# A decoder layer on one core: VectorE's next rows and mask in front of the keys' low parts, GpSimd's bias additions behind these, and tile 0's second normalisation turned on TensorE

## The chip, the core and the metric

The kernel runs on one core of a Trainium2 chip. The time is device microseconds of one execution, from its launch to its end. The core's engines work side by side, each through its own queue in order: TensorE (PE, matrix products into the eight PSUM banks; its weight loads are listed as PEld), VectorE (DVE), ScalarE (ACT), GpSimd (POOL) and SyncE (SP, which issues DMAs). They wait for one another through semaphores.

## What is computed

A decoder layer of one block-wise self-attention, one cross-attention and one feed-forward network, on `x` of 4 x 1024 x 512 and a context of 4 x 64 x 512, in fp32:

```python
x = x + self_attention(layernorm(x))        # 512-wide head, causal inside blocks of 128 rows
x = x + cross_attention(layernorm(x), ctx)  # 16 heads of 32, 64 keys, silu in place of softmax, mask
x = x + ffn(layernorm(x))                   # gelu(h @ w1 + b1) @ w2 + b2, 2048 wide

# cross-attention
q = query @ Wq.T + bq;  k = key @ Wk.T + bk;  v = value @ Wv.T + bv
scores = where(mask == 0, -1e9, q k^T * SCALE)
out = (silu(scores) @ v) @ Wo.T
```

## The kernel before

**Arithmetic.** Each fp32 operand of a product is kept as two parts, a high part (a copy in the type fp32r, written by ScalarE) and a low part (the value minus the high part, written by VectorE or GpSimd). `product` (lines 53 to 56) is three matrix instructions: high by low, low by high, high by high. So each result in a PSUM bank costs one pass of ScalarE and one of VectorE before TensorE can use it again. In names, `_hi` and `_lo` are the two parts. `*_high` and `*_low` are the functions that write them.

**Stages.** After a set-up stage, the 4096 rows go through both attentions in 8 tiles of 512 rows (`TILES`), then through the feed-forward network in 8 tiles. A tile has four blocks of 128 rows (`NB`) and the 512 columns are four chunks of 128 (`EC`).

**The attention pipeline.** `step(a, b, par)` does the self-attention of tile `a` and the cross-attention of tile `b = a - 1` together. `pipeline` writes `step(0, None, 0)` and `step(1, 0, 1)` out, runs steps 2 to 5 in a hardware loop, writes steps 6 and 7 out, and ends with `last_step(7)`. "The step of tile 2" below means a = 2, b = 1. The order on each engine is the order in which its `step` is written.

**TensorE's step.** The queries of tile b (`queries`, reading the second normalisation as `attn`); two of the four pairs of cross scores; value rows 0; the self scores (lines 1139 and 1141, which wait for the first masked cross score of tile b, `s2_masked`, and for all of `q_lo`); value rows 1; cross outputs 0 and 1 (waiting for `attn_lo`); cross scores 2 and 3; the transposes of the probabilities (line 1161); value rows 2 and 3; the probabilities times the values; cross outputs 2 and 3; the output projection; and the rows `y` of the next tile (`y_rows(a + 1, m)`, reading the next tile's first normalisation as `zT`). In step 0 the keys of all batches stand in the place of tile b's work.

**VectorE's step.** At its start, `start_step` writes the low parts of the keys (`kb_lo`, line 860), after ScalarE has written `kb_hi` (line 711). `rows_ahead` normalises the rows of tile a + 1 into `zn` (line 145). `q_low` writes the queries' low parts (line 842), `mask_now` turns the mask into floats (line 894), `values_low` writes the values' low parts (`vb_lo`, line 900), and `mask_scores` scales and masks the cross scores (line 850). ScalarE then takes `silu` of each masked score, and GpSimd subtracts (`silu_low`, line 653, `attn_lo`).

**Turning a normalisation.** TensorE needs the normalised rows with rows and columns exchanged. The kernel turns squares of 32 x 32 on VectorE (`dve.transpose`, lines 878 and 889) and moves the squares to their places by 16 DMAs (`move_squares`, line 262): for the first normalisation all are issued by SP, for the second 8 by SP and 8 by ScalarE. For tile 7's second normalisation TensorE itself does it (`transposed_rows`, line 151, 16 transposes by the identity matrix). Both parts of the second normalisation go into `attn` (lines 781 and 883).

**GpSimd's step.** The bias additions `x_in + bout_row` (line 667, four per tile), then `silu_low` for eight scores, then the reciprocal roots of the two normalisations (`norm_rstd`, lines 138 and 140). The additions start when the rows ahead are normalised (`z1_ready`); in the step of tile 1 they wait also for the keys' low parts (`kv_ready`).

## Time and profile before

| | us |
|---|---|
| median of 3 runs | 1257.65 |
| lowest and highest run | 1256.87, 1259.6 |
| the profiled execution's own time | 1257.62 |
| its span (first to last instruction) | 1255.8 |
| TensorE busy | 1230.2 |
| VectorE busy | 700.8 |
| ScalarE busy | 489.6 |
| GpSimd busy | 254.1 |
| mean granted TensorE clock, share of full speed | 0.994 |

All times in the views are microseconds from the start of the span of one profiled execution. The profiled execution is 0.03 us from the median, so what is worked out on the trace can be set against the median as it is. The attention steps run from about 40 us to 555 us, the feed-forward tiles from there to the end. In a timeline row, several instructions of a kind in a row are merged with their count, and the brackets give the idle time of the engine before the row and the instruction that ended it.

### The profile page before, as it was taken

The numbers are of one execution on the slowest core, as the hardware profiler recorded it, in microseconds if no ns is written. First come the engines' busy times: TensorE is split into PE (matmuls) and PEld (weight loads), VectorE is DVE, ScalarE is ACT, GpSimd is POOL, SyncE is SP. The second block draws the span as 40 slices with busy tenths as digits, with TensorE's granted clock in tenths as the row PEclk, the third lists the DMA queues.
The fourth block names the chain that finished last, engine by engine and source line by source line (L and its number), as shares of the span: only waits on it lengthen the run. The fifth ranks groups of instructions, "written<-read, shape, count | busy, mean of one in ns | idle before, by whom it ended". The sixth has DMA issues, their size and how long they took to land.

```text
span 1255.8 us, 15452 instructions
## 1 busy us (share of the span) xinstructions
PE 1230.2 (98%) x5560; PEld 1019.8 (81%) x5560; DVE 700.8 (56%) x1266; ACT 489.6 (39%) x888; POOL 254.1 (20%) x226
## 2 busy tenths in 40 slices
PE   9979999999999999999999999999999999999998
PEld 7867878787878788878888888888888888888887
DVE  8777878887888876855733433424424333334211
ACT  7336464646464648453332232222222222323221
POOL 2223232323232332159402001001001020010000
PEclk9999999999999999999999999999999999999999
DMA  8451515151515140325120010020100200100000
GB/s 298 148 138 33 156 35 155 33 158 36 153 34 154 38 118 13 126 92 178 50 67 1 1 68 1 1 67 0 64 3 0 67 0 0 67 0 0 35 1 33
DMA packets 76789, 82.22 MB, mean 65 GB/s; under 512 B 8257, under 2 KB 47169, under 8 KB 76737
## 3 DMA queue, kind: packets, MB, share of 16 engines
q1 hardware_dynamic: 68672, 77.90, 20.0%
q10 hardware_dynamic: 8064, 3.67, 1.3%
q8 instruction: 27, 0.44, 0.1%
q14 instruction: 26, 0.20, 0.1%
HBM read 48.51 MB, written 18.35 MB: 53 GB/s over the span
## 4 chain that ended last, share of the span: by engine, by line
PE 55%; DVE 0%; issue 0%; DVEq 0%
PE bank L54 18%; PE bank L55 18%; PE bank L56 18%; DVE resid L1403 0%; DVEq L1402 0%
## 5 line engine op out<-in xcount | busy, mean ns | idle before, releaser
L1393 DVE TENSOR_TENSOR hid_lo<-gelu_out,hid_hi 128x512 fp32r<-128x512 f32 x128 | 97.3, 760 | 405.0 <-ACT gelu_out L1357 405.0
L1353 ACT ACTIVATE hid_hi<-bank,small 128x512 fp32r<-128x512 f32 x128 | 88.0, 688 | 499.2 <-PE bank L56 499.2
L54 PE MATMUL bank<-zT,w_parts 128*128 128x512 f32 x656 | 255.5, 389 | 1.7 <-DVE zT L864 0.9
L56 PE MATMUL bank<-zT,w_parts 128*128 128x512 f32 x656 | 255.3, 389 | 0.0
L55 PE MATMUL bank<-zT,w_parts 128*128 128x512 f32 x656 | 255.3, 389 | 0.0
L54 PE MATMUL bank<-w2p_hi,hid_lo 128*128 128x512 f32 x512 | 199.3, 389 | 0.0
L55 PE MATMUL bank<-w2p_lo,hid_hi 128*128 128x512 f32 x512 | 199.3, 389 | 0.0
L56 PE MATMUL bank<-w2p_hi,hid_hi 128*128 128x512 f32 x512 | 199.2, 389 | 0.0
L54 PEld LDWEIGHTS bank<-zT,w_parts 128*128 128x128 f32 x656 | 123.1, 188 | 28.1 <-issue 2.6
L55 PEld LDWEIGHTS bank<-zT,w_parts 128*128 128x128 f32 x656 | 123.2, 188 | 25.4
L56 PEld LDWEIGHTS bank<-zT,w_parts 128*128 128x128 f32 x656 | 123.1, 188 | 25.5
L138 POOL TENSOR_SCALAR ve<-mv 128x4 f32<-128x4 f32 x24 | 7.7, 321 | 524.7 <-DVE mv L133 351.0
L56 PEld LDWEIGHTS bank<-w2p_hi,hid_hi 128*128 128x128 f32 x512 | 96.2, 188 | 19.9
L54 PEld LDWEIGHTS bank<-w2p_hi,hid_lo 128*128 128x128 f32 x512 | 96.2, 188 | 19.9
L55 PEld LDWEIGHTS bank<-w2p_lo,hid_hi 128*128 128x128 f32 x512 | 96.1, 188 | 19.9
L653 POOL TENSOR_TENSOR attn_lo<-scratch,attn_hi 128x512 fp32r<-128x512 f32 x64 | 81.6, 1296 | 139.3 <-ACT scratch L705 139.2
L1357 ACT ACTIVATE gelu_out<-bank,small 128x512 f32<-128x512 f32 x128 | 87.2, 682 | 0.0
L1390 DVE STREAM_TRANSPOSE z_cols<-zn 32x512 f32<-32x512 f32 x112 | 78.7, 703 | 4.2
L1317 POOL TENSOR_TENSOR resid<-resid,b_row 128x512 f32<-128x512 f32 x32 | 45.2, 1443 | 116.2 <-DVE zn L145 116.2
L692 ACT ACTIVATE yv_hi<-bank 128x512 fp32r<-128x512 f32 x32 | 18.9, 597 | 112.4 <-issue 85.0
L820 DVE TENSOR_TENSOR yv_lo<-bank,yv_hi 128x512 fp32r<-128x512 f32 x64 | 43.3, 685 | 32.4 <-ACT yv_hi L692 26.3
L704 ACT ACTIVATE attn_hi<-scratch 128x512 fp32r<-128x512 f32 x64 | 40.0, 624 | 40.7 <-DVE scratch L850 40.2
(156 smaller groups left out, 2039.9 us busy)
## 6 DMA issues: line engine op xcount, KB each, us to landing
x_in<-in_x SPq DMA_DIRECT2D x32, 256.0 KB, 4.8
x_dram<-resid SPq DMA_DIRECT2D x32, 256.0 KB, 2.4
raws<-in_w SPq DMA_DIRECT2D x32, 256.0 KB, 3.2
resid<-x_dram SPq DMA_DIRECT2D x32, 256.0 KB, 3.7
out_dram<-resid SPq DMA_DIRECT2D x32, 256.0 KB, 2.1
raws<-in_x SPq DMA_DIRECT2D x28, 256.0 KB, 3.5
z_cols<-raws SPq DMA_DIRECT2D x112, 64.0 KB, 2.0
z_cols<-scratch SPq DMA_DIRECT2D x56, 64.0 KB, 2.1
```

What stands on the lines that cost most here:

```text
L54: pe.matmul(out_ap, lhs[1], rhs[0], start=start, stop=False)
L55: pe.matmul(out_ap, lhs[0], rhs[1], start=False, stop=False)
L56: return pe.matmul(out_ap, lhs[0], rhs[0], start=False, stop=stop)
L653: pool.tensor_tensor(attn[1][:, j % 4, :], act_in[:, j % 3, :], f(attn[0][:, j % 4, :]), ALU.subtract).then_inc(attn_lo, 1)
L692: act.activation(yv[0][:, m, :], bank[y_bank(a, m)][:, :], ACT.Copy).then_inc(y_hi, 1)
L704: act.activation(attn[0][:, j % 4, :], act_in[:, j % 3, :], ACT.Silu)
L820: dve.tensor_tensor(hl[1][:, m, :], bank[from_bank][:, :], f(hl[0][:, m, :]), ALU.subtract).then_inc(made, 1)
L1317: pool.tensor_tensor(resid[:, slot, i, :], resid[:, slot, i, :], b2_row[:, :], ALU.add).then_inc(x2_biased, 1)
L1353: act.activation(hid[0][:, c % 4, :], bank[4 + c % 3][:, :], ACT.Gelu, bias=b1_col[:, c:c + 1])
L1357: act.activation(gelu_out[:, c % 2, :], bank[4 + c % 3][:, :], ACT.Gelu, bias=b1_col[:, c:c + 1]).then_inc(hid_full, 1)
L1390: dve.transpose(*squares(TURNS_AT_ONCE * (c - FIRST_TURN) + n, z3_cols)).then_inc(z3_turned, 1)
L1393: dve.tensor_tensor(hid[1][:, c % 4, :], gelu_out[:, c % 2, :], f(hid[0][:, c % 4, :]), ALU.subtract).then_inc(hid_lo, 1)
```

## The change

Four things change.

1. In VectorE's step for every tile b, `rows_ahead` (while there is a next tile) and `mask_now` come ahead of `start_step`, and `values_low` comes between `q_low(2)` and `q_low(3)`. Before, this held for the step of tile 1 alone as far as `rows_ahead` and the mask go, and there `values_low` stood behind the first three masked scores.
2. GpSimd's bias additions wait in every step for the keys' low parts.
3. Tile 0's second normalisation is turned by 16 transposes on TensorE, after `y_rows(1, 1)`, into banks 7, 5, 0 and 1. ScalarE and VectorE write its two parts from there. The turning on VectorE and the 16 DMAs of SP and ScalarE go away for this tile. The semaphore counts of the moves and turns shift by one tile.
4. In step 0 `z1_low` (the low parts of tile 1's first normalisation) comes before the statistics of the second normalisation.

GpSimd's step:

```diff
                             if more(a):
                                 pool.wait_ge(z1_ready, NB * (a + 2))
-                                if b is not None and first(b):
-                                    pool.wait_ge(kv_ready, HEADS_PER_CHUNK)
+                                if b is not None:
+                                    pool.wait_ge(kv_ready, len(BLOCKS) * b + HEADS_PER_CHUNK)
```

ScalarE's step, after the first normalisation's high parts (SP's step has the same condition around its half of `move_squares`):

```diff
-                                act.wait_ge(z2_turned, NB * (a + 1))
-                                move_squares(act, scratch, range(QUADS // 2, QUADS), z2_moved)
+                                if not first(a):
+                                    act.wait_ge(z2_turned, NB * a)
+                                    move_squares(act, scratch, range(QUADS // 2, QUADS), z2_moved)
                                 y_high(a + 1, 0)
                                 y_high(a + 1, 1)
-                                act.wait_ge(z2_moved, MOVES * (a + 1))
-                                for c in range(EC):
-                                    act.activation(by_blocks(attn[0], c), by_quads(c), ACT.Copy).then_inc(z2T_hi, 1)
+                                if first(a):
+                                    for i in range(NB):
+                                        act.wait_ge(z2T_done, i + 1)
+                                        act.activation(attn[0][:, :, cols(i)], chunks(bank[FIRST_Z2_BANK[i]][:, :]),
+                                                       ACT.Copy).then_inc(z2T_hi, 1)
+                                else:
+                                    act.wait_ge(z2_moved, MOVES * a)
+                                    for c in range(EC):
+                                        act.activation(by_blocks(attn[0], c), by_quads(c), ACT.Copy
+                                                       ).then_inc(z2T_hi, 1)
```

VectorE, `rows_ahead` and the step:

```diff
                         def rows_ahead(n, b):
+                            if b is not None and first(b):
+                                dve.wait_ge(z2T_done, NB)
                             norm_rows(dve, lambda i: ahead[i], mv1, rstd1, ln1, n)
...
                             if b is not None:
-                                if first(b):
+                                if more(a):
                                     rows_ahead(a + 1, b)
-                                    mask_now(b)
+                                mask_now(b)
                                 start_step(b)
-                                if more(a) and not first(b):
-                                    rows_ahead(a + 1, b)
-                                q_low(b, 0)
-                                q_low(b, 1)
-                                if not first(b):
-                                    mask_now(b)
-                                q_low(b, 2)
-                                if not first(b):
-                                    values_low(b)
+                                for m in range(EC - 1):
+                                    q_low(b, m)
+                                values_low(b)
                                 q_low(b, EC - 1)
                                 dve.wait_ge(mask_ready, b + 1)
                                 for j in range(3):
                                     mask_scores(b, j)
-                                if first(b):
-                                    values_low(b)
...
+                            if first(a):
+                                for c in range(EC):
+                                    z1_low(1, c)
                             dve.wait_ge(x1_ready, NB * (a + 1))
...
                                 norm_rows(dve, lambda i: x1_rows(i, par), mv2, rstd2, ln2, a)
-                                turn2(a, b)
-                                if b is not None:
+                                if not first(a):
+                                    turn2(a, b)
...
-                                for c in range(EC):
-                                    z2_low(a, c)
+                                if first(a):
+                                    for i in range(NB):
+                                        dve.wait_ge(z2T_hi, i + 1)
+                                        dve.tensor_tensor(attn[1][:, :, cols(i)],
+                                                          chunks(bank[FIRST_Z2_BANK[i]][:, :]),
+                                                          f(attn[0][:, :, cols(i)]), ALU.subtract).then_inc(z2T_lo, 1)
+                                else:
+                                    for c in range(EC):
+                                        z2_low(a, c)
```

TensorE's step, at its end, with the new table of banks:

```diff
+FIRST_Z2_BANK = (7, 5, 0, 1)
...
                                 for m in range(EC):
                                     y_rows(a + 1, m)
+                                    if first(a) and m == 1:
+                                        pe.wait_ge(keys_out, EC)
+                                        for i in range(NB):
+                                            transposed_rows(pe, z2_ready, a, i, FIRST_Z2_BANK[i], z2T_done)
```

The order on VectorE at the start of the step of tile 6; `zn` are the rows ahead, `qo` the queries, `scratch` the masked scores. Before:

```order
L860 TENSOR_TENSOR kb_lo<-keys_now,kb_hi 32x4x64 x4
L145 TENSOR_SCALAR zn<-raws,mv,rstd 128x512 x4
L842 SCALAR_TENSOR_TENSOR qo_hi<-bank,bias_cols,qo_hi 64x512
L842 SCALAR_TENSOR_TENSOR qo_lo<-bank,bias_cols,qo_lo 64x512
L842 SCALAR_TENSOR_TENSOR qo_hi<-bank,bias_cols,qo_hi 64x512
L842 SCALAR_TENSOR_TENSOR qo_lo<-bank,bias_cols,qo_lo 64x512
L894 TENSOR_SCALAR mask_i<-mask_i 128x512
L842 SCALAR_TENSOR_TENSOR qo_hi<-bank,bias_cols,qo_hi 64x512
L842 SCALAR_TENSOR_TENSOR qo_lo<-bank,bias_cols,qo_lo 64x512
L900 TENSOR_TENSOR vb_lo<-values_now,vb_hi 64x4x32 x4
```

The same place now:

```order
L146 TENSOR_SCALAR zn<-raws,mv,rstd 128x512 x4
L904 TENSOR_SCALAR mask_i<-mask_i 128x512
L869 TENSOR_TENSOR kb_lo<-keys_now,kb_hi 32x4x64 x4
L851 SCALAR_TENSOR_TENSOR qo_hi<-bank,bias_cols,qo_hi 64x512
L851 SCALAR_TENSOR_TENSOR qo_lo<-bank,bias_cols,qo_lo 64x512
L851 SCALAR_TENSOR_TENSOR qo_hi<-bank,bias_cols,qo_hi 64x512
L851 SCALAR_TENSOR_TENSOR qo_lo<-bank,bias_cols,qo_lo 64x512
L851 SCALAR_TENSOR_TENSOR qo_hi<-bank,bias_cols,qo_hi 64x512
L851 SCALAR_TENSOR_TENSOR qo_lo<-bank,bias_cols,qo_lo 64x512
L910 TENSOR_TENSOR vb_lo<-values_now,vb_hi 64x4x32 x4
```

The four row normalisations and the mask moved from behind the keys' low parts to ahead of them; in both orders the last `q_low` and the masked scores follow.

The order on ScalarE at the end of step 0; `yv_hi` are tile 1's rows `y`, `attn_hi` the second normalisation of tile 0. Before:

```order
L769 ACTIVATE raws<-bank,bias_cols 128x4x64 x4
L262 DMA z_cols<-scratch 32x4x128 x8
L692 ACTIVATE yv_hi<-bank 128x512 x2
L781 ACTIVATE attn_hi<-z_cols 128x512 x4
L692 ACTIVATE yv_hi<-bank 128x512 x2
```

Now:

```order
L770 ACTIVATE raws<-bank,bias_cols 128x4x64 x4
L693 ACTIVATE yv_hi<-bank 128x512 x2
L784 ACTIVATE attn_hi<-bank 128x4x128 x4
L693 ACTIVATE yv_hi<-bank 128x512 x2
L712 ACTIVATE kb_hi<-keys_now 32x4x64 x8
```

The eight DMAs left the queue, and the four copies read PSUM banks that TensorE's transposes fill.

## Rows read from the trace of the kernel before

**Rows 1.** The page, busy time of TensorE: busy us, share of span, instructions.

```profile
PE 1230.2 (98%) x5560; PEld 1019.8 (81%) x5560; DVE 700.8 (56%) x1266; ACT 489.6 (39%) x888; POOL 254.1 (20%) x226
```

**Rows 2.** Waits of TensorE: waited-for instruction, us in total, times, longest.

```profile
PE bank L1139 <- DVE scratch L850: 9.8, 5, 2.0
```

**Rows 3.** Timeline of TensorE: start, us, instruction, idle time before it in brackets.

```profile
76.54 0.47 PE L54 MATMUL bank<-zT,w_parts 128*128 128x512 f32 x1 [0.87 <-DVE zT L864]
...
93.82 0.80 PE L54 MATMUL bank<-attn_hi,w_parts 128*128 128x512 f32 x1 [6.15 <-DVE attn_lo L883]
...
119.70 0.50 PE L54 MATMUL bank<-attn_hi,vb_lo 128*128 128x512 f32 x1 [0.44 <-POOL attn_lo L653]
...
124.55 0.63 PE L1161 MATMUL bank<-ident,scratch 128*128 128x128 f32 x4 [1.34 <-DVE yv_lo L820]
...
175.82 0.38 PE L1139 MATMUL bank<-zT,yv_hi 128*128 128x256 f32 x1 [1.99 <-DVE scratch L850]
```

**Rows 4.** Stretches of TensorE: window, length, busy (count), granted clock, DMA, GB/s.

```profile
93.82:97.82 4.00, 4.00 (x9) 0.50 0.00 0
175.82:181.12 5.30, 5.30 (x33) 0.68 0.10 37
239.14:242.88 3.74, 3.74 (x32) 1.00 0.16 59
301.08:306.38 5.30, 5.30 (x32) 0.68 0.10 39
485.99:489.63 3.64, 3.64 (x33) 1.00 0.04 13
516.52:518.18 1.66, 1.66 (x17) 1.00 0.83 309
```

**Rows 5.** Timeline of VectorE, step of tile 2.

```profile
159.08 0.69 DVE L820 TENSOR_TENSOR yv_lo<-bank,yv_hi 128x512 fp32r<-128x512 f32 x1 [0.69 <-ACT yv_hi L692]
162.60 1.76 DVE L860 TENSOR_TENSOR kb_lo<-keys_now,kb_hi 32x256 fp32r<-32x256 f32 x4 [2.83 <-ACT kb_hi L711]
164.39 1.92 DVE L145 TENSOR_SCALAR zn<-raws,mv,rstd 128x512 f32<-128x512 f32 x4
...
172.16 1.24 DVE L900 TENSOR_TENSOR vb_lo<-values_now,vb_hi 64x128 fp32r<-64x128 f32 x4
...
174.99 1.89 DVE L850 SCALAR_TENSOR_TENSOR scratch<-bank,mask_i 128x512 f32<-128x512 f32 x3
```

**Rows 6.** Timeline of ScalarE, step of tile 2.

```profile
159.08 3.49 ACT L711 ACTIVATE kb_hi<-keys_now 32x256 fp32r<-32x256 f32 x8
...
167.48 0.68 ACT L716 ACTIVATE qo_lo<-bank,bias_cols 64x512 fp32r<-64x512 f32 x1
...
170.05 0.68 ACT L716 ACTIVATE qo_lo<-bank,bias_cols 64x512 fp32r<-64x512 f32 x1
```

**Rows 7.** Timeline of GpSimd, step of tile 2.

```profile
166.48 5.23 POOL L667 TENSOR_TENSOR x_in<-x_in,bout_row 128x512 f32<-128x512 f32 x4 [9.60 <-DVE zn L145]
```

**Rows 8.** Timeline of VectorE and GpSimd, end of tile 0's step.

```profile
68.47 2.48 DVE L987 TENSOR_TENSOR resid<-bank,x_in 128x512 f32<-128x512 f32 x4
...
73.92 2.47 DVE L864 TENSOR_TENSOR zT<-z_cols,zT 128x512 fp32r<-128x512 f32 x4
76.31 1.91 DVE L145 TENSOR_SCALAR zn<-resid,mv,rstd 128x512 f32<-128x512 f32 x4
...
74.75 1.33 POOL L140 TENSOR_TENSOR rstd<-ve,minus_half 128x4 f32<-128x4 f32 x1
```

**Rows 9.** Timeline of VectorE and GpSimd, step of tile 1.

```profile
96.89 0.43 DVE L894 TENSOR_SCALAR mask_i<-mask_i 128x512 f32<-128x512 int32 x1
...
111.02 4.17 DVE L900 TENSOR_TENSOR vb_lo<-values_now,vb_hi 64x128 fp32r<-64x128 f32 x4
...
111.17 3.87 POOL L653 TENSOR_TENSOR attn_lo<-scratch,attn_hi 128x512 fp32r<-128x512 f32 x3 [6.93 <-ACT scratch L705]
```

**Rows 10.** Timeline of ScalarE, tile 7's second normalisation.

```profile
517.15 2.07 ACT L156 ACTIVATE zT<-bank 128x512 fp32r<-128x512 f32 x4 [8.00 <-PE bank L151]
```

More of the change, by code:

```diff
@@ L629, in step @@
                                 load_kv(0)
-                            if more(a):
-                                sp.wait_ge(z2_turned, NB * (a + 1))
+                            if more(a) and not first(a):
+                                sp.wait_ge(z2_turned, NB * a)
                                 move_squares(sp, scratch, range(QUADS // 2), z2_moved)
@@ L642, in last_step @@
                         def last_step(b):
-                            sp.wait_ge(z2_moved, MOVES * (TILES - 1))
+                            sp.wait_ge(z2_moved, MOVES * (TILES - 2))
                             for c in range(STAGES):
@@ L785, in step @@
                                 for i in range(NB):
-                                    transpose_high(act, i, BLOCK_BANK[i], z2T_done, z2T_hi, 0)
+                                    transpose_high(act, i, BLOCK_BANK[i], z2T_done, z2T_hi, 1)
                         def last_step(b):
@@ L873, in turn2 @@
                             dve.wait_ge(z2_ready, NB * (a + 1))
-                            if b is not None:
-                                dve.wait_ge(attn_lo, PAIRS * (b + 1))
+                            dve.wait_ge(attn_lo, PAIRS * (b + 1))
                             dve.nop(nofuse=True)
@@ L999, in step @@
                             if more(a):
-                                for c in range(EC):
-                                    z1_low(a + 1, c)
+                                if not first(a):
+                                    for c in range(EC):
+                                        z1_low(a + 1, c)
                                 norm_rows(dve, lambda i: x1_rows(i, par), mv2, rstd2, ln2, a)
-                                turn2(a, b)
-                                if b is not None:
+                                if not first(a):
+                                    turn2(a, b)
                                     for i in range(3):
@@ L1015, in step @@
                                 y_low(a + 1, 1)
-                                for c in range(EC):
-                                    z2_low(a, c)
+                                if first(a):
[5 more added lines that the diff above has]
+                                else:
+                                    for c in range(EC):
+                                        z2_low(a, c)
                                 y_low(a + 1, 2)
@@ L1032, in last_step @@
                             start_step(b)
-                            dve.wait_ge(z2T_done, NB)
+                            dve.wait_ge(z2T_done, 2 * NB)
                             norm_rows(dve, lambda i: x_in[:, i, :], mv3, rstd3, ln3, 0)
```

## The prediction

> **What bounds the kernel now.** I read the page first. TensorE is busy 1230.2 of 1255.8 us [rows 1], so only its idle time, and time at a lower clock, can be won. Next come its waits: the longest entry is 9.8 us in 5 waits for `scratch` of line 850, the masked cross scores [rows 2]. The timeline places the others: one wait of 6.15 us for `attn_lo` of line 883, the low part of tile 0's second normalisation, 0.87 us ahead of tile 1's rows `y`, and 0.44 and 1.34 us in the step of tile 1 [rows 3]. All other idle time lies in the set-up, in tile 0's transposes of probabilities, in the last step and behind the feed-forward tiles, where nothing is changed. Last I read the clock by stretches. After the 6.15 us of waiting, nine products take 4.00 us at a granted clock of 0.50, which is the 1.2 GHz level. The self scores behind the waits of tiles 2 and 4 take 5.30 us at a mean of 0.68. The same instructions behind the wait of tile 3 take 3.74 us at 1.00 (2.4 GHz), and in tile 7, with no wait, 3.64 us [rows 4]. Tiles 5 and 6 read like tile 3.
>
> **Why the five waits are there.** In the step of tile 2, TensorE is free at 175.82 - 1.99 = 173.83 and the first masked score starts at 174.99 [rows 3, 5]. It comes late since VectorE is a full queue from 162.60 on: low parts of the keys, then 1.92 of rows ahead, `q_low` in eight halves with the mask among them, 1.24 of `vb_lo`. Ahead of 162.60 it idles for 2.83 us, waiting for ScalarE's `kb_hi` [rows 5, 6].
>
> **Part 1, rows ahead and mask first.** They go into that hole: 1.92 for the rows and 0.43 for the mask, which is its price with GpSimd idle [rows 5, 9]. That is 2.35 of 2.83, so `kb_lo` still starts at 162.60 and ends at 164.36. What it needs, the rows' factors from GpSimd, is in place earlier than 159.8: GpSimd has been idle for 9.60 us when its bias additions start at 166.48, since 156.9 [rows 7]. Behind `kb_lo` stand six halves of `q_low`. Two of them lie between 172.16 + 1.24 = 173.40 and 174.99, so one takes 0.79 [rows 5]. They wait for ScalarE's halves too: the sixth of these ends at 167.48 + 0.68 = 168.16, at 0.7 each the first at 164.6 [rows 6]. So VectorE's six end at 164.6 + 6 x 0.79 = 169.3. `vb_lo` takes 1.24, to 170.6, ScalarE's last half is there at 170.05 + 0.68 = 170.73 [rows 6], and the last two `q_low` end at 172.1 to 172.3. The first masked score then starts near 172.2 in place of 174.99, and is done 0.7 later, at 172.9. TensorE comes at 173.83. The wait of 1.99 is gone with about 0.9 to spare, in five steps: **9.8 us**. Everything behind it on VectorE, ScalarE and GpSimd is earlier by about 2.8, TensorE by 2.0, so no later wait of these steps can open that was closed before: in the undisturbed steps of tiles 3, 5 and 6 TensorE waits nowhere else.
>
> **Part 2, GpSimd's additions behind the keys.** They start at 164.4 in place of 166.48, since what they wait for is done earlier than before. They end at 164.4 + 5.1 = 169.5 [rows 7], ahead of the first silu. What they can hit is `vb_lo`: 1.24 alone, but 4.17 with GpSimd's subtractions beside it [rows 5, 9]. `vb_lo` starts at 169.3 and the additions end at 169.5, so I take 0.2 to 0.7 of delay, within the 0.9 to spare. Zero on the path.
>
> **Part 3, clock.** With no wait the self scores of tiles 2 and 4 cost 3.64 in place of 5.30, and those of tiles 3, 5 and 6 3.64 in place of 3.74 [rows 4]: 2 x 1.66 + 3 x 0.10 = **3.6 us**.
>
> **Part 4, tile 0's second normalisation.** The wait of 6.15 goes. TensorE pays 16 transposes: 1.66 for the same instructions in tile 7 [rows 4], and 0.1 for the slower product behind them: net **4.4 us**. Is it ready in time? `z1_low` (2.47) now stands right behind the residual additions, which end at 68.47 + 2.48 = 70.95, and ends at about 73.4. Statistics, aggregates and GpSimd's factors follow, all later by `z1_low`'s 2.4. The factors ended at 74.75 + 1.33 = 76.08 and so end at 78.5, and the normalised rows (1.91) lie at 78.6 to 80.5 [rows 8]. TensorE starts the rows `y` at 76.54 - 0.87 = 75.67, with 48 products to 93.82 - 6.15 = 87.67, or 0.232 each, so two chunks end at 81.2. The rows are there, with 0.7 to spare. The transposes end at 82.9. ScalarE copies 4 x 0.5 (2.07 [rows 10]) to about 84.1, VectorE subtracts (2.5, as in [rows 8]) to about 86.7, and TensorE wants them at 87.67 - 0.87 + 1.76 = 88.56. Slack 1.9. ScalarE no longer issues eight DMAs there, SP neither; nothing stands behind these in SP's queue but the next tile's. Nine products at half clock (4.00) become 9 x 0.232 = 2.09: **1.9 us**.
>
> **Part 5, `z1_low` first.** The rows of `zT` are ready at 73.4 and TensorE is free at 75.67: **0.9 us**.
>
> **Part 6, the step of tile 1.** Its `vb_lo` took 4.17 beside GpSimd's subtractions, and held up the turning, the self scores' masking and so on to the wait of 1.34 [rows 3, 9]; the other steps, with `vb_lo` early, have no such wait, nor the one of 0.44. From 88.56 on this step runs as that of tile 2 does: **1.8 us**.
>
> **Sum.** 9.8 + 3.6 + 4.4 + 1.9 + 0.9 + 1.8 = 22.4. Against the profiled execution, 1257.62 - 22.4 = 1235.2; the median is the same within 0.03, so I say **1235.3 us**. The feed-forward part does not change.
>
> **Bounds.** The transposes: from 1.66, if the product behind them loses nothing, to 1.66 + 1.9, if nine products behind them run at half clock. The first product behind a wait took 0.47 to 0.80 [rows 3] where a row of products further on takes less; that each wait gone gives back some 0.08 more is not in the sum and is worth up to 0.5. The scores' wait: from zero to 0.5 us in each of six steps, if `vb_lo` is held longer than I take. The spread of the runs before is -0.8 to +1.9 us.
>
> **Rivals.**
>
> A. *The transposes lower the clock.* At their stretch in tile 7 the clock was 1.00 [rows 4], and TensorE is busy before and behind. For it speaks that waits of 2.0 were followed by half clock in two of five cases. Price: the nine products behind them, 1.9, or these and the transposes at half clock, 1.9 + 1.7: 1237.2 to 1238.9. Chance 0.08. The Trainium skill ("TensorE: Matmul & The Clock Gate", Part 4: PE-mode transpose) says that the full clock does not engage for transposes, which would make this rival the likely one; the 1.00 in tile 7 is against it.
>
> B. *The port contention takes the gain.* If GpSimd's additions and all four `vb_lo` collide, these take 4.17, 2.9 more, the first masked score is done at 175.7 and the waits of 1.9 and the half clock return, now in the step of tile 1 too: 22.4 - 9.8 - 3.6 - 1.9 = 7.1 saved, 1250.5. It takes an overlap of 4 us; I work out 0.2. A part of it, 0.5 to 1 us of wait in six steps, gives 1238 to 1241. Chance 0.10 for both.
>
> C. *Slower: VectorE stands in front of the rows ahead.* `rows_ahead` waits for GpSimd's factors. Now the keys' low parts, the queries' and the scores stand behind it. If the factors come s after 159.8, the first masked score slips by s less 0.5 (hole) less 0.9 (spare). With six such steps the 22.4 are used up at s = 22.4 / 6 + 1.4 = 5.1, that is factors at 164.9 in place of 156.9; at 166 the time is 1257.6 + 6 x 1.1 = 1264. The 2.9 us by which the factors are early speak against it. Chance 0.02.
>
> D. *The gap is not VectorE's.* If the self scores' wait ended by something else, the 13.4 of parts 1 and 3 stay: 1248.7. The row names line 850, and in tile 7, where there are no rows ahead, the same place has no wait [rows 4]. Chance 0.02.
>
> **How the numbers follow.** The forecast has 0.78, and 1233.8 to 1240 holds it, A, and the small half of B: 1233.8 is the sum less 0.8 (the runs), 0.1 (transposes) and 0.5 (first products), 1240 the sum with 0.5 us in six steps and the spread of the runs. A measurement of this kernel tells about 0.2% (2.5 us) from no change. Only C gives slower: 0.02. Same needs B with a clock worse than seen: 0.01. Faster 0.97.
>
> **What would show it.** TensorE's waits have no entry for the masked scores of line 859, and none for the second normalisation of tile 0. The granted clock stays 1.00 from 40 us to the end. On VectorE the rows ahead and the mask start right behind the last `y_low`, `kb_lo` has 0.3 to 0.5 of idle time before it, and the first masked score starts 12.3 behind the end of `y_low` in place of 15.2. The additions of GpSimd start with the end of `kb_lo`. Sixteen transposes stand between the second and third chunk of rows `y`. Wrong would be: `vb_lo` over 2 us in the loop, a wait of TensorE at the transposes, or a new wait behind the masked scores.

## The result, and the profile after

The changed kernel takes **1236.68 us** in the median of 4 runs (1235.93 to 1237.49), beside 1257.72 for the kernel before: a ratio of 0.983 with an interval of 0.982 to 0.9845. The profiled execution took 1236.69, its span 1234.6. Set beside [rows 1], the page begins:

```profile
span 1234.6 us, 15467 instructions
PE 1225.1 (99%) x5576; PEld 1017.9 (82%) x5576; DVE 692.1 (56%) x1262; ACT 489.5 (40%) x888; POOL 250.2 (20%) x226
```

TensorE's view of waits (engine and tile, what ended the wait, microseconds in total, times, longest), which answers [rows 2]:

```profile
PE bank L56 <- issue: 1.7, 2, 0.8
PE bank L470 <- POOL kb_lo L432: 1.3, 1, 1.3
PE bank L55 <- POOL attn_lo L654: 1.0, 2, 0.6
PE bank L55 <- DVE attn_lo L893: 1.0, 1, 1.0
```

The wait for the masked scores (line 859 now) has no entry any more, and neither has tile 0's second normalisation. Two entries are new: `attn_lo` of line 893, once, and `issue`, twice. The second means that TensorE stood and the profile shows nothing that it waited for.

TensorE's timeline, beside [rows 3]: the 16 transposes in tile 0's step, the product behind them, and two of the three new gaps. Brackets hold the idle time ahead and what ended it.

```profile
81.32 1.91 PE L152 MATMUL bank<-ident,zn 128*128 128x128 f32 x16
82.98 0.48 PE L55 MATMUL bank<-zT,w_parts 128*128 128x512 f32 x1
...
208.91 0.50 PE L55 MATMUL bank<-attn_hi,w_parts 128*128 128x512 f32 x1 [0.97 <-DVE attn_lo L893]
...
797.09 0.40 PE L56 MATMUL bank<-zT,w_parts 128*128 128x512 f32 x1 [0.84 <-issue]
```

The third, at 972.19, is like the second, with 0.82. VectorE and then GpSimd in the step of tile 2, the place of [rows 5] and [rows 7]:

```profile
149.53 1.91 DVE L146 TENSOR_SCALAR zn<-raws,mv,rstd 128x512 f32<-128x512 f32 x4
151.63 0.43 DVE L904 TENSOR_SCALAR mask_i<-mask_i 128x512 f32<-128x512 int32 x1 [0.19 <-DVE zn L146]
152.45 1.76 DVE L869 TENSOR_TENSOR kb_lo<-keys_now,kb_hi 32x256 fp32r<-32x256 f32 x4 [0.39 <-ACT kb_hi L712]
...
159.18 1.33 DVE L910 TENSOR_TENSOR vb_lo<-values_now,vb_hi 64x128 fp32r<-64x128 f32 x4
...
162.10 1.89 DVE L859 SCALAR_TENSOR_TENSOR scratch<-bank,mask_i 128x512 f32<-128x512 f32 x3
```

```profile
154.37 5.04 POOL L668 TENSOR_TENSOR x_in<-x_in,bout_row 128x512 f32<-128x512 f32 x4 [7.29 <-DVE kb_lo L869]
```

The values' low parts take 1.33, 0.1 over their 1.24 alone, so GpSimd's additions hardly touch them. The first masked score starts at 162.10 and TensorE starts the self scores at 163.66 without a wait.

**Where the 21.2 us of span went.** The listed idle time undercounts a wait, because the ends of the pipelined products are modelled. So I measured from the start of one group of products to the start of the next. "Attention" is from the first product of tile 0's step (line 336 or 337, at about 40 us) to the first of the feed-forward part (line 578 or 579). "Feed-forward" is from there to the end of the span.

| | before | after | saved | forecast |
|---|---|---|---|---|
| values 0 ahead of the self scores, five steps (4.87, 4.85, 4.86, 4.86, 4.74; now 2.72) | | | 10.6 | 9.8 |
| self scores (5.30 twice and 3.74 three times; now 3.64) | | | 3.6 | 3.6 |
| tile 0: rows `y` and transposes | 17.28 | 12.69 | 4.6 | 4.4 |
| tile 0: queries at half clock | 12.91 | 10.88 | 2.0 | 1.9 |
| tile 0: wait ahead of rows `y` | 1.15 | 0.12 | 1.0 | 0.9 |
| step of tile 1 (0.74, 1.52, 0.16, 0.29) | | | 2.7 | 1.8 |
| end of the step of tile 2 (10.88, now 12.01; queries +0.14) | | | -1.3 | 0 |
| **attention, whole** | 515.57 | 491.91 | 23.7 | 22.4 |
| **feed-forward** | 699.92 | 701.98 | -2.1 | 0 |
| set-up | 40.31 | 40.67 | -0.4 | 0 |

The rows of the attention stretch add up to 23.2; the other 0.5 lies in pieces under 0.12. 23.7 - 2.1 - 0.4 = 21.2.

### The profile page after: what moved, and what is told of

Its sections match the earlier page's. It is cut to its first block, busy times and chain, and to the rows that moved or that the text cites. A ratio compares the mean times of both kernels' runs of the same rounds, so it can differ in the third digit from the quotient of the medians.

```text
span 1234.6 us, 15467 instructions
## 1 busy us (share of the span) xinstructions
PE 1225.1 (99%) x5576; PEld 1017.9 (82%) x5576; DVE 692.1 (56%) x1262; ACT 489.5 (40%) x888; POOL 250.2 (20%) x226
## 3 DMA queue, kind: packets, MB, share of 16 engines
q10 hardware_dynamic: 6912, 3.15, 1.1%
## 4 chain that ended last, share of the span: by engine, by line
PE 56%; DVE 0%; issue 0%; DVEq 0%
PE bank L55 19%; PE bank L57 19%; PE bank L56 19%; DVE resid L1420 0%; DVEq L1419 0%
## 5 line engine op out<-in xcount | busy, mean ns | idle before, releaser
L55 PE MATMUL bank<-w_parts,zT 128*128 128x512 f32 x128 | 51.3, 401 | 0.0
```

The source lines that it names most:

```text
L55: pe.matmul(out_ap, lhs[1], rhs[0], start=start, stop=False)
```

## Experiments

All kernels together: the median, the ratio to the kernel before with its interval, the two stretches as defined above, and the idle gaps of TensorE inside the feed-forward part.

| kernel | median | ratio | attention | feed-forward | gaps |
|---|---|---|---|---|---|
| before | 1257.72 | | 515.57 | 699.9 | none |
| after | 1236.68 | 0.982-0.9845 | 491.91 | 702.0 | 0.84, 0.82 |
| c1_after | 1236.12 | 0.9795-0.9831 | 491.99 | 702.5 | 1.26, 0.94 |
| e1_order_only | 1241.17 | 0.9836-0.9871 | 499.98 | 700.0 | none |
| e2_tile0_only | 1251.65 | 0.9927-0.9961 | 507.97 | 702.4 | 1.01, 0.77 |
| e3_no_gp_wait | 1254.19 | 0.9945-0.9975 | 508.79 | 702.2 | 0.93, 0.85 |
| e4_rows_behind | 1245.14 | 0.9884-0.9917 | 500.21 | 702.1 | 1.01, 0.50 |
| e5_mask_behind | 1238.74 | 0.9836-0.9869 | 493.38 | 702.1 | 0.77, 0.74 |
| e6_values_late | 1254.56 | 0.9965-0.9987 | 509.68 | 702.4 | 1.19, 0.74 |
| e7_transposes_twice | 1235.39 | 0.9806-0.9839 | 493.19 | 700.0 | none |
| e8_z1_low_late | 1237.61 | 0.9812-0.9859 | 492.50 | 702.4 | 1.01, 1.04 |
| b1_value_rows_early | 1236.08 | 0.9797-0.9843 | 491.37 | 702.2 | 0.77, 0.76 |
| b2_shifted | 1233.70 | 0.9783-0.9822 | 490.74 | 700.1 | none |
| b3_both | 1242.21 | 0.9841-0.9885 | 490.85 | 710.6 | 3.15, 2.73 |

**c1_after**: after once more.

> The changed kernel once more. What the first trace had that the prediction had not: a wait of 0.97 us of TensorE for tile 2's second normalisation (208.9), and two idle stretches of 0.84 and 0.82 us in the feed-forward loop that no semaphore ended (795.9 and 971.0), some 3 us in all from start to start. Theory 'of this kernel': the same three stand at the same places and cost the same. Theory 'of the execution': they stand elsewhere, or not at all, and the span differs by what is missing. Time 1236 to 1238 in both.

The new wait came back in the same place (1.05 at 209.42), and the two gaps too. They belong to the program, not to one execution.

**e1_order_only** is before with parts 1, 2 and 6 alone, **e2_tile0_only** has parts 4 and 5 alone.

```diff
-                                if b is not None and first(b):
-                                    pool.wait_ge(kv_ready, HEADS_PER_CHUNK)
+                                if b is not None:
+                                    pool.wait_ge(kv_ready, len(BLOCKS) * b + HEADS_PER_CHUNK)
...
+                                for m in range(EC - 1):
+                                    q_low(b, m)
+                                values_low(b)
```

> The kernel before with VectorE's new order in all steps and GpSimd's wait alone; tile 0's second normalisation goes by VectorE and DMAs as before. Theory of the prediction: the five waits of the self scores go (10.6 us from start to start), their clock loss (3.6), and the two waits in the step of tile 1 (2.3), so 16.5 less than before: 1241.2. TensorE still waits 6.15 us for tile 0's second normalisation, with nine products at half clock. Rival (the waits of tile 1's step hang on tile 0's late start, not on values_low): these stay, 1243.5. Rival (gain given back behind the scores): a new entry of several us in TensorE's waits, 1246 or more.

> The changed kernel with VectorE's old order and GpSimd's old wait; only tile 0's normalisation on TensorE and the earlier z1_low are left. Theory of the prediction: 6.4 + 1.9 + 1.0 less 1.7 for the transposes: 7.6 less than before, 1250.1; the five waits of about 2 us and the two in tile 1's step stay. Rival (the transposes lower the clock): granted clock of 0.5 behind 81 us, 1252. Rival (half clock in two tiles of five hangs on the place in time): the tiles with half clock behind their wait are others than tiles 2 and 4, 1248.5 to 1252 by their number.

The order alone takes 15.6 off the attention stretch (forecast 9.8 + 3.6 + 1.8 = 15.2), tile 0's edits 7.6 (forecast 4.4 + 1.9 + 0.9 = 7.2). The sum, 23.2, is nearly the 23.7 of both, so the two halves add up. That the first lies so near its forecast is partly luck. From start to start, 1.05 of its 15.6 comes from a place without an edit: tile 0's wait is 5.07 in place of 6.15, since the moves ahead of it land earlier. In tile 4's step it loses 1.9 again, to the wait below. The second median is 1.5 over what was expected: it has the gaps of after (2.5 more in its feed-forward part), which tile 0's edit brings and the order does not. Its self scores take 5.31 in tiles 2 and 4 and 3.72 to 3.75 in tiles 3, 5 and 6. So half clock stands in the same two tiles as before, though these run 7.4 us earlier, and the rival of the place in time did not come true.

In e1_order_only one wait for a masked score is left, 0.99 at 291.40, in tile 4's step alone. It starts on VectorE:

```profile
278.48 1.92 DVE L145 TENSOR_SCALAR zn<-raws,mv,rstd 128x512 f32<-128x512 f32 x4 [2.61 <-issue]
```

**e3_no_gp_wait**: after, without GpSimd's wait for the keys' low parts.

```diff
-                                if b is not None:
-                                    pool.wait_ge(kv_ready, len(BLOCKS) * b + HEADS_PER_CHUNK)
```

> The changed kernel without GpSimd's new wait: the bias additions start when the rows ahead are there, beside the mask and the keys' low parts. Theory 'shared port': the mask takes 0.9 in place of 0.43, kb_lo up to 4.2 in place of 1.76, the first masked score slips by up to 2.4, TensorE waits up to 1.4 us in six steps: 1240 to 1246. Rival 'no contention at this place' or 'GpSimd is the one that is held': kb_lo 1.8, the same time as the changed kernel, 1236.7.

Contention it is, but at almost twice the highest price expected (17.5 in the median against 9.3): the attention stretch is 16.9 longer, more than the 15.6 that the new order brings. VectorE, GpSimd and TensorE's waits:

```profile
154.88 1.56 DVE L902 TENSOR_SCALAR mask_i<-mask_i 128x512 f32<-128x512 int32 x1 [0.19 <-DVE zn L146]
156.37 4.82 DVE L867 TENSOR_TENSOR kb_lo<-keys_now,kb_hi 32x256 fp32r<-32x256 f32 x4
161.22 0.74 DVE L849 SCALAR_TENSOR_TENSOR qo_hi<-bank,bias_cols,qo_hi 64x512 fp32r<-64x512 f32 x1
```

```profile
154.87 5.59 POOL L666 TENSOR_TENSOR x_in<-x_in,bout_row 128x512 f32<-128x512 f32 x4 [4.55 <-DVE zn L146]
```

```profile
PE bank L1150 <- DVE scratch L857: 7.6, 6, 1.3
PE bank L1092 <- DVE qo_lo L849: 4.0, 11, 0.4
```

The mask takes 1.56 in place of 0.43 and the keys' low parts 4.82 in place of 1.76: 4.2 more per step, against about 0.9 of spare. TensorE now waits twice in a step, for the queries' low parts (0.3 to 0.4 at a time) and for the masked score (1.3), and loses 2.5 to 3.0 per step from start to start in six steps. I had looked for the first masked score alone.

The Trainium skill ("SBUF — State Buffer", section "SBUF: two separate sides") says that VectorE and GpSimd share one pair of ports, taken for a whole instruction, for VectorE's operations with two inputs in SBUF among them. The rows agree: the keys' low parts, with two such inputs, stretch by 2.7 times, while the queries' halves, with one of their two large inputs in a PSUM bank, take 0.74 to 0.76 with or without GpSimd.

**e4_rows_behind** and **e5_mask_behind**: the two pieces of part 1 put back one at a time.

```diff
-                                if more(a):
-                                    rows_ahead(a + 1, b)
                                 mask_now(b)
                                 start_step(b)
+                                if more(a):
+                                    rows_ahead(a + 1, b)
```

```diff
-                                mask_now(b)
                                 start_step(b)
...
                                 q_low(b, 1)
+                                mask_now(b)
                                 q_low(b, 2)
```

> After, but VectorE's rows ahead stand behind the start of the step's keys' low parts' successors as before the change; the mask stays in front, GpSimd's additions stay behind the keys. If the hole ahead of the keys' low parts is what pays (my Part 1), the 1.92 of rows ahead are back in VectorE's full queue: the first masked score of tile 2 starts about 1.9 to 2.4 later than in after, TensorE waits about 1.0 for it in the five steps of tiles 2 to 6 (half of the 1.99 of before, since the mask's 0.43 and the contention are gone), 5 x 1.0 to 1.2 and up to 2 for a lower clock: 1242 to 1245. If the gain came from GpSimd's additions being moved away alone, there is no wait and the time stays at 1236 to 1237.

> After, but the mask stands again between the second and third half of the queries' low parts; rows ahead stay in front. The mask then runs beside GpSimd's additions and should take 0.9 to 1.5 in place of 0.43. If there are 0.9 of spare ahead of the masked scores as I worked out, the wait for them is 0 to 0.3 in six steps: 1236 to 1238. If there is no spare left, each of six steps loses the whole 0.9 to 1.5: 1242 to 1245.

With the rows ahead behind the keys, VectorE stands 2.50 idle ahead of `kb_lo` again, and TensorE waits 6.4 in six steps for the masked scores (1.26 to 1.47 from start to start in five of them, 0.55 in tile 3's): 8.3 on the attention stretch, and a median of 1245.14, at the upper end of what was expected. So the hole ahead of the keys carries a good half of the order's 15.6. The clock stays at 1.00 behind these waits.

The mask beside the additions takes 0.84 in place of 0.43:

```profile
157.66 0.84 DVE L904 TENSOR_SCALAR mask_i<-mask_i 128x512 f32<-128x512 int32 x1
```

The first masked score then starts 0.83 later, at 162.93. No wait is listed, yet values 0 take 2.79 to 2.91 in place of 2.72 in five of the six steps, and the self scores behind them 3.72 to 3.75 in place of 3.65: 0.2 to 0.3 per step. With smaller pieces the attention stretch is 1.5 longer, and the median is 0.7 over the expected range. Of the delay of 0.83, 0.1 to 0.2 reaches TensorE's start of the self scores, so the spare that I put at 0.9 is about 0.7 (an estimate).

**e6_values_late**: the values' low parts behind three masked scores in all steps, as the step of tile 1 had it before.

```diff
-                                for m in range(EC - 1):
+                                for m in range(EC):
                                     q_low(b, m)
-                                values_low(b)
-                                q_low(b, EC - 1)
...
+                                values_low(b)
```

> After, but the values' low parts (1.33) stand behind the three masked scores, where GpSimd's subtractions of the silu run, in all steps, as in before they stood in the step of tile 1 alone. If two-input operations on VectorE stretch beside GpSimd, they take about 4.2, and the waits of before's step of tile 1 (0.44 and 1.34, 0.60 and 1.52 from start to start) come up in all seven steps with a predecessor: 7 x 1.8 to 2.1, 1249 to 1251. If that step was late for another reason (its place behind tile 0), the time stays at 1236 to 1238.

```profile
166.18 4.19 DVE L910 TENSOR_TENSOR vb_lo<-values_now,vb_hi 64x128 fp32r<-64x128 f32 x4
```

```profile
166.33 3.88 POOL L654 TENSOR_TENSOR attn_lo<-scratch,attn_hi 128x512 fp32r<-128x512 f32 x3 [4.11 <-ACT scratch L706]
```

Here they are 4.19 beside GpSimd's subtractions, and the pair of waits of tile 1's step (0.46 and 1.28) stands in all six steps. That confirms the cause of part 6. The time is above the expectation, which counted seven steps at 1.8 to 2.1: six lose 2.8 to 3.0 each from start to start. The transposes of the probabilities (+0.2) and the value rows behind them (+0.3) are slower too.

**e7_transposes_twice**: tile 0's 16 transposes done twice.

> After, but TensorE does the 16 transposes of tile 0's second normalisation twice, the second set writing the same values again. What transposes cost is 1.66 for sixteen, if the granted clock stays at 1.00 over 32 of them in a row: 1236.7 + 1.7 = 1238.3, nothing waits, since what needs them has 1.9 of slack and loses 1.7. If the clock falls in transposes (rival A), nine products behind them at half clock or these and the transposes: 1240.2 to 1243.5, and the records show 0.50 there.

TensorE by windows (length, busy and count of each engine, then the granted clock, DMA share, GB/s): the 32 transposes, then the 24 products behind them.

```profile
81.92:85.33 3.41, 3.41 (x33) 3.41 (x32) 3.02 (x9) 1.62 (x4) 1.01 (x2) 1.00 0.67 239
85.33:90.90 5.57, 5.57 (x27) 4.59 (x26) 2.78 (x5) 1.64 (x4) 0.26 (x1) 1.00 0.00 0
```

The second set costs 1.75, at a clock of 1.00 (2.4 GHz) in and behind them: rival A is out, and the sentence of the Trainium skill that spoke for it ("TensorE: Matmul & The Clock Gate", Part 4: PE-mode transpose) does not hold for these 32. But the kernel, expected at 1238.3, is no slower than after (1235.39 against 1236.68). The attention stretch is 1.3 longer, and the two gaps of the feed-forward part, where nothing had been touched, are gone. This led to the next kernel.

**b2_shifted**: 32 empty instructions in TensorE's program.

```diff
                                 for m in range(EC):
+                                    if first(a):
+                                        for k in range(8):
+                                            pe.wait_ge(x1_ready, 1 + k % NB)
+                                            pe.nop(nofuse=True)
                                     y_rows(a + 1, m)
```

> After, with 32 empty instructions more in TensorE's program, each with a wait that is already met, eight ahead of each chunk of rows y in tile 0's step. They do nothing; all of TensorE's program behind them stands 32 instructions further on. Seen so far: the feed-forward part (from its first product to the end of the span) takes 699.9 to 700.0 in before, in the kernel with the new order only, and in the kernel with the transposes doubled, and 702.0 to 702.5 with two idle stretches of 0.5 to 1.3 and instruction fetches beside them in the six kernels whose TensorE program is that of after. Theory: what decides is where the loop over the feed-forward tiles stands in the program. Shifted by 32, as with the doubled transposes, it takes 700.0, the two idle stretches are gone, and the time is 1236.5 - 2.1 = 1234.4, plus at most 1 for the empty instructions. Rival: the transposes' doubling helped in another way (less collision of transfers): then 702.1 and 1236.5 to 1237.5.

The fastest kernel: 1233.70 (1232.99 to 1234.35), 2.9 of span below after, where 2.1 were expected. Both gaps are gone, and so is the new wait of 1.0 at the end of tile 2's step. The DMA view around the gap at 797, of after (785 to 812) and then of b2_shifted (784 to 811, the same place in its feed-forward part); the columns are packets, MB, and share of the 16 engines:

```profile
q8 instruction: 4, 0.07, 0.9%
```

```profile
q8 instruction: 1, 0.02, 0.3%
```

Over the whole run q8, which brings instructions, has 27 packets in before and in e1_order_only, 28 in e7_transposes_twice and b2_shifted, and 46 in all the others, whose loop over the feed-forward tiles fetches its code on every pass. The gaps end 264.5 and 439.6 behind the start of the part, 175 apart: that is the length of one pass (two tiles), so there is one behind each jump back to the loop's head. TensorE's branch at the loop's end stands in the view of its line, of b2_shifted and then of after (how often, the least, median and most ns of one, and the first and last start; the last of the three is not taken):

```profile
L1288 PEldq COMPARE_BRANCH  x3: 76/213/233, 788.8 to 1137.0; - x3
L1284 PEldq COMPARE_BRANCH  x3: 83/3475/3507, 789.9 to 1140.1; - x3
```

A jump back takes 0.21 to 0.23 us in the kernels without gaps and 3.3 to 3.9 in all the others. In after, one packet of q8 comes during it (at 790.99) and one ahead of the gap (794.76). TensorE takes the branch 4.0 ahead of the first product of the new pass, which starts at 793.82, so the 3.5 hold up no product there but leave 0.5 of the lead. The gap comes ten products later. It does so in the nine kernels whose loop has the place of after, and two products into the pass in b3_both, whose loop stands 16 instructions (eight products with their weight loads) further on. So the gap keeps its place in TensorE's program, not its place in the loop.

The Trainium skill ("Runtime: NRT & Kernel Launch", section "Instruction fetch mechanics") says that TensorE's instruction memory holds 2048 instructions, filled in blocks of 256 (the packets of q8 are of 16 KB each here), and that a taken branch waits for a fetch when its target is not in the window of two blocks. The 3.3 to 3.9 agree with a wait for a fetch. The two blocks do not agree with the kernels without gaps: between 787 and 1159 in b2_shifted q8 brings nothing, while TensorE jumps back over more than six blocks twice. An estimate from the page's block: the loop has 768 products, as many weight loads and 38 others, 1574 or 6.15 blocks, so by where it starts it touches 7 or 8 of the 8. Counted with the weight loads, the loop stands 33 instructions later in after than in before and in e1_order_only, 49 later in b3_both, and 65 later in b2_shifted and e7_transposes_twice. The two places between are the bad ones, and an eighth block would be touched from 37 places in every 256, which fits. So does the gap's fixed place. If a block ends there, an estimate from the products and the shifts puts that end some 22 instructions into the loop in after and 6 in b3_both (eight blocks touched), 55 in before and ahead of the loop with the shift of 32 (seven touched). The blocks' limits themselves no view shows, nor which block is thrown out.

**b3_both** has 16 empty instructions in place of 32 and the edit of **b1_value_rows_early**, which in tile 0's step rounds value rows 0 right behind the self scores.

```diff
+                            if b is None:
+                                act.wait_ge(s1_done, 2)
+                                v_high(a, 0)
...
+                            if b is None:
+                                v_low(a, 0)
```

> The two small gains together: tile 0's value rows of the first block split earlier (by 0.5 to 0.6) and 16 empty instructions in TensorE's program in place of 32. The loop of the feed-forward part has 768 products, with their weight loads, and 38 other instructions. If a shift by 16 already brings it to a good place, the part takes 700.0 and the time is 1233.8 to 1234.2; if not, 702.1 and 1235.8 to 1236.3. Which of the two can't be told beforehand: it is two to three in favour of the good place.

> After, but in tile 0's step ScalarE rounds the value rows of the first block right behind the self scores, and VectorE subtracts their low part while ScalarE takes the exponentials. If the wait of 0.45 at the turning of tile 0's probabilities comes from VectorE having that subtraction ahead of it, it goes, with 0.15 more from start to start: 1235.6 to 1236.1. If ScalarE's exponentials become the last, 0.6 later by the rounding ahead of them, nothing is won or 0.3 lost: 1236.5 to 1237.

The 16 do not help: they make it worse. TensorE's row and window at the first gap:

```profile
796.85 0.59 PE L57 MATMUL bank<-zT,w_parts 128*128 128x512 f32 x1 [3.15 <-issue]
```

```profile
796.85:802.00 5.15, 5.15 (x13) 3.98 (x13) 0.00 (x0) 0.68 (x2) 0.00 (x0) 0.50 0.69 201
```

The gap is 3.15 and the 13 products behind it run at 0.50, the 1.2 GHz level. The feed-forward part takes 710.6, and my odds of two to three for the good place were a miss. So was the price of the bad one (702.1). Why one bad place costs 2 and the other 10 can be read from start to start. The jump back takes as long here as in after (3.56 and 3.63), but only two products are left to run ahead of the gap in place of ten, which is 1.8 less cover each time. The two gaps cost 3.3 and 2.9 where those of after cost 1.0 each, and the products behind them at the lower clock another 2.8 and 1.6. b1 alone removes the wait of 0.45 in tile 0's step and 0.54 from the attention stretch, as expected. The medians can't tell 0.5 us, and b1 with the shift by 32 was not run.

**e8_z1_low_late**: part 5 undone.

```diff
-                            if first(a):
-                                for c in range(EC):
-                                    z1_low(1, c)
...
-                                if not first(a):
-                                    for c in range(EC):
-                                        z1_low(a + 1, c)
+                                for c in range(EC):
+                                    z1_low(a + 1, c)
```

> After, but in tile 0's step the low parts of the next turned rows stand behind the statistics again, as in before. If Part 5 of the prediction is right, TensorE waits 0.9 for them ahead of tile 1's rows y (0.87 in before): 1237.4 to 1237.7. The second normalisation then is 2.5 earlier and waits for nothing. If it had been GpSimd or the transposes that removed this wait, the time stays at 1236.5.

```profile
76.33 0.47 PE L55 MATMUL bank<-zT,w_parts 128*128 128x512 f32 x1 [0.87 <-DVE zT L873]
```

The wait is back at 0.87, 1.03 from start to start; 0.5 of it is given back at the wait of tile 2, which is shorter here (0.43).

## Why the prediction was right

1236.68 was measured and 1235.3 forecast. The mechanisms named were the ones at work. The attention stretch gave 1.3 more than the 22.4 of the sum, and the set-up and the feed-forward part, which I had left at zero, took 2.5 back. That the two lie only 1.4 apart is partly luck: the terms of the sum, with the small pieces, came out 2.6 larger than I said, and three losses that I had put at nothing (1.3, 2.1 and 0.4) took 3.8.

**Part 1.** The row order held. `kb_lo` has 0.39 of idle ahead (0.3 to 0.5 said), the first masked score starts 12.48 behind the end of `y_low` (12.3 said), the wait is gone in five steps. The term was mis-sized: 9.8 of listed idle is 10.6 from start to start. The prediction had named this (0.08 a wait, up to 0.5) and left it out; it is 0.16 a wait. e4_rows_behind and e5_mask_behind show that the hole and the 0.7 of spare are real. The step's last sentence failed: "no later wait of these steps can open that was closed before". One did, 0.97 at 208.91, at the end of tile 2's step.

That wait is not VectorE's order: e2_tile0_only, with the old order, has it too (0.62), and e1_order_only, with the new one, has none there. The eight moves of squares on ScalarE's queue read there:

```profile
196.16 6.61 ACTq L263 DMA_DIRECT2D z_cols<-scratch  x8
```

In b2_shifted:

```profile
196.31 5.47 ACTq L263 DMA_DIRECT2D z_cols<-scratch  x8
```

In after an instruction fetch (q8) lies between the moves, at 200.0, and about 1 us with hardly any traffic follows. In b2_shifted the fetch comes as the moves begin, they are 1.1 faster and no wait opens. Over the attention steps of all fourteen traces, ScalarE's eight moves take 5.17 to 5.55 where no fetch starts among them and 5.47 to 6.76 where one does. In the nine kernels whose TensorE program has the place of after, the fetch comes 3.9 behind the first move of tile 2's step, the moves take 6.08 to 6.76, and TensorE waits 0.43 to 1.10. But the place alone does not decide. e7_transposes_twice has the same shift of 32 and the fetch at the same point as b2_shifted (0.2 behind the first move), and there the moves take 6.17 and TensorE waits 0.52. So that a fetch delays the moves is an inference that fits all traces; what it costs is not settled, and no run tried it by itself.

**Part 2** was right on its own question (`vb_lo` 1.33, additions from 154.37, at the end of `kb_lo`) and wrong in what it priced. I asked what the additions would hit in their new place and not what they would hit in the old one. Without GpSimd's wait they meet the mask and the keys' low parts, and e3_no_gp_wait loses 16.9 where the order brings 15.6. The wait "at zero on the path" is the condition for part 1.

**Part 3** came out as said, 3.6. The clock is 1.00 over the whole attention stretch. Of the 3.6, only 3.3 is clock: the 3.74 of tile 3 stood at 1.00 already [rows 4], so its 0.10 belongs to the wait ahead of it.

**Parts 4 and 5.** 4.6 for 4.4, 2.0 for 1.9, 1.0 for 0.9. The transposes start at 81.32 (81.2 said), the rows for them end at 80.0, the low parts end at 83.97 + 2.47 = 86.44 (86.7 said), and the queries start at 88.54 (88.56 said). So the slack is 2.1 for the 1.9 said. The second set of transposes in e7_transposes_twice opened no wait, but it does not try the slack as its expectation had it: it holds back TensorE's queries as well, which start at 90.90, 3.5 behind the end of the low parts at 87.42.

**Part 6.** Cause right (e6_values_late), size wrong: 2.7 for 1.8. I took the two listed waits (0.44 and 1.34). From start to start they are 0.74 and 1.52, and the transposes and value rows behind them were 0.16 and 0.29 slower.

**Outside the sum.** "The feed-forward part does not change" failed: +2.1. I reasoned from what its engines do and wait for; what changed was where its loop stands in TensorE's program.

**Rivals.** A is excluded by e7_transposes_twice. B did not occur, since the wait of part 2 holds the additions back; e3_no_gp_wait shows its mechanism at other instructions, the mask and the keys' low parts, with a price of 17. C has no trace in after. Its mechanism, VectorE standing in front of the rows ahead, is seen once, in e1_order_only's step of tile 4 (2.61), and there the row names `issue`, not GpSimd's factors: two packets of q14, the other queue that brings instructions, come at about 276.5 and 279, and the loop of the attention steps begins its second pass there. In after this queue has 20 packets in the whole run in place of 26, none at this step. That the fetch held VectorE was not tried by itself. D is excluded by e1_order_only.

## What to carry over

Put what can run early into the hole where the engine waits for another's first result, and hold back the neighbour that slows it: here the order without that wait brought nothing (the wait without the order was not run). Size a removed wait from start to start of the work around it, not by the listed idle. When a program with a hardware loop grows or shrinks, look at the branch at the loop's end, at the gap behind each jump back, and at the packets of the instruction queues: here 32 empty instructions ahead of it gave back 2 us, and 16 cost 8 more.

## What the runs showed that I had not expected

- The place of a loop in TensorE's program, with the same instructions in it, costs 0 (before, and after shifted by 32), 2.1 to 2.5 (after), or 10.6 us (after shifted by 16) in a part of 700.
- Thirty-two empty instructions with met waits between products cost TensorE nothing that shows: the attention stretch of b2_shifted is 1.17 shorter than that of after, and its rows `y` of tile 1 take what they took.
- Idle stretches of 1.1 to 1.3 never lowered the granted clock (six times in e3_no_gp_wait, five in e4_rows_behind). Of the five of 1.85 to 1.99 in before [rows 4], two did, and of the four of 1.86 to 1.98 in e2_tile0_only again two, in the same tiles; 3.15 and 2.73 did in b3_both.
- A `tensor_scalar` on integers with one large input, the mask, stretched beside GpSimd too: 0.43 alone, 0.84 and 1.56 beside the additions.
